# A two-layer graph network on one core: the running sums and the destination rows move from HBM into SBUF

## The reference

```python
# layer 0: attention
xl = h @ Wl + bl;  xr = h @ Wr + br;  e = edge_weight1 @ We
logits = leaky_relu(xl[src] + xr[dst] + e, 0.2) @ att
ex = exp(logits - segment_max(logits, dst)[dst]);  den = segment_sum(ex, dst)
out = segment_sum(xl[src] * (ex / den[dst])[:, None], dst)
h0 = batchnorm(gelu(h + out + bias));  x = x + h0
# layer 1: messages
em = relu(layernorm(concat(h[src], h[dst]) @ msg_w + msg_b)) * edge_weight
messages = segment_sum(em, dst) / count
x = x + gate * relu(layernorm(concat(h, messages) @ upd_w)) + (1 - gate) * h
```

## Time and profile before

| | |
|---|---|
| median of 3 runs | 2326.95 us (2321.8 to 2328.92) |
| profiled execution, own time | 2325.57 us |
| its span, first to last instruction | 2323.7 us |
| PE busy | 1608.6 us, 69% |
| DVE busy | 1539.4 us, 66% |
| ACT busy | 1027.0 us, 44% |
| POOL busy | 1646.2 us, 71% |
| moved by DMA | 233.58 MB |

### The profile page before, as it was taken

The page is one execution under the profiler, slowest core; times in us unless marked ns, Lnnn a source line. Parts: engine busy times, 40 slices in busy tenths (PEclk is TensorE's granted clock), DMA queues, the critical chain, the costliest instruction groups (busy, mean ns, idle before and its releaser), DMA issues.

```text
span 2323.7 us, 45075 instructions
## 1 busy us (share of the span) xinstructions
PE 1608.6 (69%) x10064; PEld 1151.3 (50%) x10064; DVE 1539.4 (66%) x5042; ACT 1027.0 (44%) x3827; POOL 1646.2 (71%) x1729
## 2 busy tenths in 40 slices
PE   5588787777777777777676776656566656656564
PEld 4366454555545555555465554444444444445443
DVE  6667665656565555655568886776666667676757
ACT  4444443444444444434454554444444444444435
POOL 5677777777777777777037777777777777777753
PEclk9799999999999999999778898998989899898997
DMA  8633333333333333333652343333333333333324
GB/s 222 181 99 98 96 96 88 96 89 95 88 96 92 93 95 88 95 88 77 158 166 70 98 106 96 87 95 87 95 87 94 91 91 86 93 96 88 93 63 111
DMA packets 222657, 233.58 MB, mean 101 GB/s; under 512 B 116266, under 2 KB 166332, under 8 KB 222533
## 3 DMA queue, kind: packets, MB, share of 16 engines
q0 software_dynamic: 55168, 114.83, 20.1%
q1 hardware_dynamic: 165958, 117.37, 18.8%
q10 hardware_dynamic: 1472, 0.73, 0.2%
HBM read 196.29 MB, written 36.46 MB: 100 GB/s over the span
## 4 chain that ended last, share of the span: by engine, by line
POOL 53%; issue 20%; PE 11%; DVE 7%; DMA 6%; ACT 1%; POOLq 1%; SPq 1%; DVEq 0%; ACTq 0%
POOL room L697 53%; DMA room<-src_table,rec 3%; PE psum L951 2%; PE psum L878 2%; PE psum L956 1%; PE psum L969 1%; DMA dst_table<-rows 1%; PE psum L778 1%; PE psum L860 1%; PE psum L850 1%; PE psum L843 1%; DMA room<-state 1%; DVE stats L1352 1%; DVE rows L1364 0%; PE psum L868 0%
## 5 line engine op out<-in xcount | busy, mean ns | idle before, releaser
L697 POOL DMA_INDIRECT room<-src_table,rec x1638 | 1573.8, 961 | 523.8 <-issue 486.1
L951 PE MATMUL psum<-room,ident 128*128 128x384 f32 (+1 forms) x512 | 273.1, 619 | 370.5 <-DMA room<-src_table,rec 313.9
L1242 ACT ACTIVATE room<-psum 128x128 f32<-128x128 f32 x832 | 219.0, 274 | 541.4 <-DVE room L1778 538.8
L1592 DVE TENSOR_TENSOR room<-psum,room 128x384 f32<-128x384 f32 (+1 forms) x256 | 151.2, 591 | 386.9 <-ACT room L1174 216.3
L1174 ACT ACTIVATE room<-psum 128x384 f32<-128x384 f32 (+1 forms) x256 | 131.8, 515 | 523.2 <-PE psum L850 516.9
L1778 DVE TENSOR_TENSOR room<-psum,msg_g 128x384 f32<-128x384 f32 (+1 forms) x256 | 151.0, 590 | 275.9 <-PE psum L956 267.6
L951 PEld LDWEIGHTS psum<-room,ident 128*128 128x128 f32 x512 | 85.7, 210 | 404.0 <-issue 363.7
L969 PE MATMUL psum<-room 128*125 128x128 f32 x1664 | 264.4, 302 | 1.6 <-ACT room L1254 1.6
L878 PE MATMUL psum<-room 128*125 128x128 f32 x1664 | 254.0, 293 | 16.5 <-ACT room L1192 10.6
L956 PEld LDWEIGHTS psum<-room 125*128 125x128 bf16 x2496 | 185.9, 108 | 129.5 <-issue 107.5
L1792 DVE SCALAR_TENSOR_TENSOR room<-room,rstd_e,msg_beta 128x128 f32<-128x128 f32 x832 | 242.5, 349 | 10.2
(11 more groups left out here) (224 smaller groups left out, 2228.6 us busy)
## 6 DMA issues: line engine op xcount, KB each, us to landing
room<-dst_perm SPq DMA_DIRECT2D x128, 416.0 KB
room<-src_table,rec POOLq DMA_INDIRECT x1638
room<-dst_table SPq DMA_DIRECT2D x128, 64.0 KB
src_table<-rows SPq DMA_DIRECT2D x24, 224.0 KB
dst_table<-rows SPq DMA_DIRECT2D x24, 224.0 KB
st_in<-state SPq DMA_DIRECT2D x64, 65.5 KB
st_in<-state SPq DMA_DIRECT2D x64, 64.0 KB
state<-st_out SPq DMA_DIRECT2D x64, 64.0 KB
```

What stands on the lines that cost most here:

```text
L697: pool.indirect_dma_start(out=xg[:, u, t * P:(t + 1) * P], out_offset=None, in_=table[:, :], in_offset=bass.IndirectOffsetOnAxis(ap=rec[:, ...
L951: nc.tensor.matmul(msg_bank[b][:, cols], ident[:, :], xg[:, u, t0 * P:t1 * P], start=True, stop=False, skip_group_check=True)
L1242: i = nc.scalar.activation(sq[:, j * P:(j + 1) * P], msg_bank[b][:, j * P:(j + 1) * P], ACT.Square, accum_out=var_e[:, c, j:j + 1])
```

## The change

- Nodes are laid out so that node n lies in partition n mod 125, column n / 125 (`(t p)` in place of `(p t)`). A window that begins at any node is then two neighbouring columns, split at a partition: the partitions from `left` on lie in the first column, those below it in the second.
- Destination rows stay in SBUF (`dst_rows`), and `dst_table` is gone. DVE picks the window out of the two columns (`nodes_of`, `pick_rows`), with a start column that it reads into a register.
- The states stay in SBUF (`held`, `held_den`, `held_max`, `cnt`), and `state0`, `state1`, `factor_rows`, their zeroing, their loads and stores and the reading back are gone. DVE merges into both columns (`gat_merge`, `gat_add`, `msg_add`). `held` shares its room with `feat_h`, so it is set to zero on POOL before loop 1 and on DVE before loop 2.
- `split_low` comes in block 2, not 3; the masks are written as bf16; the node's own part enters by transposes of `node_h`.
- At the end TensorE puts the own part into banks (`own_in_bank`) in another order around the wait for the last state: groups 2 and 3 into banks that the loop leaves free, 0 and 1 once DVE and ACT are through with theirs, 4 and 5 behind the first transposes of the sums.
- The chunk list has nine more small steps a block; x, x1, the source table and the output move in pieces of 512 bytes.

```diff
             def store_rows(n, g):
                     sp.dma_start(node_cols(src_table[n], p0, p1, t0, t1),
-                                 rows[p0:p1, g % 3, 0, 0:t1 - t0, :]).then_inc(s_src_out[g % 3], 16)
-                for p0, p1 in NODE_ROWS:
-                    sp.dma_start(node_cols(dst_table[n], p0, p1, t0, t1),
-                                 rows[p0:p1, g % 3, 1, 0:t1 - t0, :]).then_inc(s_dst_out[g % 3], 16)
+                                 rows[p0:p1, g % 3, 0:t1 - t0, :]).then_inc(s_src_out[g % 3], 16)
...
-            return table[0:N, :].rearrange("(p t) f -> p t f", t=NT)[p0:p1, t0:t1, :]
+            return table[0:N, :].rearrange("(t p) f -> p t f", p=PP)[p0:p1, t0:t1, :]
...
+            done = 10 * GT * PP
+            pool.wait_ge(s_proj, 10)
+            pool.memset(feat_room[:, 0:done], 0.0).then_inc(s_zero, 1)
+            pool.wait_ge(s_proj, NG)
+            pool.memset(feat_room[:, done:NC * D], 0.0).then_inc(s_zero, 1)
...
+            def start_of(u):
+                return starts_of(pair_info[0:1, u, 1:2])[0]
+            def nodes_of(s, k, u):
+                v = u % 2
+                base, left = (pair_info[:, u, i:i + 1].bitcast(F32) for i in (2, 3))
+                dve.wait_ge(s.dst[v], turns(s, k, v, 2, 32, last))
+                dve.tensor_scalar(side[:, u, 0:1], iota_p[:, :], left, None, ALU.is_ge)
+                dve.tensor_scalar(side[:, u, 1:2], iota_p[:, :], left, None, ALU.is_lt).then_inc(s.side, 1)
+                dve.wait_ge(s.side, k + 1)
+                dve.tensor_scalar(turned[:, :], side[:, u, 1:2], float(W), base, ALU.mult, ALU.add).then_inc(s.turned, 1)
...
+                dve.tensor_tensor(node_id[:, v:v + 1], turned[:, :], iota_p[:, :], ALU.add).then_inc(s.id, 1)
+            def pick_rows(s, k, u, start):
...
+                dve.tensor_scalar(dfar[0:W, :], rows_of[1], side[0:W, u, 1:2], None, ALU.mult).then_inc(s.far, 1)
+                dve.wait_ge(s.far, k + 1)
+                dve.scalar_tensor_tensor(out=dwin[0:W, v, :], in0=rows_of[0], scalar=side[0:W, u, 0:1], in1=dfar[0:W, :],
+                                         op0=ALU.mult, op1=ALU.add).then_inc(s.win, 1)
...
-            def msg_add(k, u):
+            def msg_add(k, u, start):
-                dve.wait_ge(s.st[v], turns(s, k, v, 2, 16, last))
+                dve.tensor_tensor(fac2[0:W, :], factor[:, bass.ds(start, 2)], side[0:W, u, :], ALU.mult).then_inc(s.fac, 1)
                 dve.wait_ge(s.sum, nth(k, NB))
-                dve.wait_ge(s_fac[v], (k - v) * 8 + 16)
-                dve.scalar_tensor_tensor(out=st_out[0:W, v, 0:D], in0=sum_bank[v][0:W, 0:D], scalar=fac_in[0:W, v:v + 1],
-                                         in1=st_in[0:W, v, 0:D], op0=ALU.mult, op1=ALU.add).then_inc(s.state, 1)
...
+                for j in range(2):
+                    rows_j = held[:, bass.ds(start + j, 1), :].rearrange("p a f -> p (a f)")
+                    i = dve.scalar_tensor_tensor(out=rows_j, in0=sum_bank[v][0:W, 0:D], scalar=fac2[0:W, j:j + 1],
+                                                 in1=rows_j, op0=ALU.mult, op1=ALU.add)
+                i.then_inc(s.state, 1)
...
-            for u in range(2):
-                sp.wait_ge(gat.kept[u], (last + U) * 8)
-                settle(sp)
-            for q, (t0, t1) in enumerate(PIECES):
-                for p0, p1 in NODE_ROWS:
-                    sp.dma_start(st_all[p0:p1, t0:t1, :], node_cols(state0, p0, p1, t0, t1)).then_inc(s_x[q], 16)
...
-            for g in range(NZ):
+            for g in (2, 3):
                 own_in_bank(g)
+            pe.wait_ge(msg.hg, nth(last + U, 0))
+            pe.wait_ge(msg.sq, nth(last + U, 0))
+            for g in (0, 1):
+                own_in_bank(g)
+            pe.wait_ge(msg.state, last + U)
             turn_msg(0)
+            turn_msg(1)
+            for g in (4, 5):
+                own_in_bank(g)
...
+            dve.wait_ge(s_u, NG)
+            dve.memset(feat_room[:, :], 0.0).then_inc(s_zero, 1)
```

More of the change, by code:

```diff
@@ L535, in slot @@
+                    two, three = two_chunks(k + 2)
                     if there(k, -3, end):
@@ L1260, in msg_slot @@
                     lagged(msg_relu, k, u, b, 1, end)
-                    if b == 0 and there(k, -1, end):
+                    if b == 1 and there(k, -1, end):
                         split_high(msg, k + 1, (u + 1) % U)
@@ L1503, in list_block, with step @@
-                dve.wait_ge(s_blk2, kb + 1)
+                steps = [0]
+                def step(i):
+                    steps[0] += 1
+                    i.then_inc(s_blk1, 1)
+                    dve.wait_ge(s_blk1, kb * LIST_STEPS + steps[0])
+                ge(dve, s_blk, kb * 2)
+                step(dve.tensor_scalar(hit, ends, k_col[:, :], None, ALU.is_le, ALU.add, accum_out=lcol[:, 0:1]))
+                step(dve.scalar_tensor_tensor(out=hit2, in0=iota_c[:, :], scalar=lcol[:, 0:1], in1=first, op0=ALU.is_equal,
+                                              op1=ALU.mult, accum_out=lcol[:, 1:2]))
@@ new lines, in list_block @@
+                step(dve.scalar_tensor_tensor(out=lcol[:, 2:3], in0=k_col[:, :], scalar=float(W), in1=lcol[:, 1:2],
+                                              op0=ALU.mult, op1=ALU.add))
+                dve.tensor_scalar(k_col[:, :], k_col[:, :], float(P), None, ALU.add).then_inc(s_blk, 1)
+                start, turn, left, off = (lcol[:, i:i + 1] for i in range(3, 7))
+                step(dve.tensor_scalar(start, lcol[:, 2:3], float(N), None, ALU.min))
+                step(dve.tensor_scalar(turn, start, 1.0 / W, None, ALU.mult))
@@ L1634, in gat_add @@
+                for j in range(2):
+                    rows_j = held[:, bass.ds(start + j, 1), :].rearrange("p a f -> p (a f)")
+                    dve.scalar_tensor_tensor(out=rows_j, in0=rows_j, scalar=eshift[0:W, j:j + 1], in1=part[0:W, j, :],
+                                             op0=ALU.mult, op1=ALU.add)
                 dve.drain().then_inc(s.state, 1)
             def gat_slot(k, u, end):
+                now = (u - 2) % U
                 for b in range(NB):
@@ L1640, in gat_slot @@
                     lagged(gat_max, k, u, b, 1, end)
+                    if b == 0 and there(k, -1, end):
+                        nodes_of(gat, k + 1, (u + 1) % U)
+                        pick_rows(gat, k + 1, (u + 1) % U, start_of((u + 1) % U))
                     if b == 1 and there(k, 2, end):
-                        gat_merge(k - 2, (u - 2) % U)
+                        start = start_of(now)
+                        gat_merge(k - 2, now, start)
                     if there(k, -1, end):
@@ L1680, in batch_stats @@
                 i.then_inc(s_bnst, 1)
-            done = 0
-            for q in range(NQ):
-                attention(q)
-                while done < NG and t_end(done) <= PIECES[q][0]:
-                    batch_stats(done)
-                    done += 1
-            for g in range(done, NG):
-                batch_stats(g)
+            dve.wait_ge(gat.state, last + U)
+            settle(dve)
+            link(dve.tensor_scalar(factor[:, :], held_den[:, :], 1e-16, None, ALU.add))
+            link(dve.reciprocal(factor[:, :], factor[:, :]))
+            link(dve.scalar_tensor_tensor(out=factor[:, :], in0=held_max[:, :], scalar=BIG / 10, in1=factor[:, :], op0=ALU.is_lt,
+                                          op1=ALU.mult))
+            for g in range(NG + 2):
+                if g < NG:
+                    attention(g)
+                if g >= 2:
+                    batch_stats(g - 2)
             dve.wait_ge(s_bnst, NG)
```

409 lines of the change are left out of this document (190 added, 219 removed).

## The result

The changed kernel takes 2299.59 us (median of 4 runs, 2296.81 to 2302.73), the kernel before 2327.39 (2321.8 to 2328.92): a ratio of 0.9878, 95% interval 0.9864 to 0.9891. Its profiled execution took 2299.76 us, with a span of 2297.9. The gathers first: page, part 5, and the timeline of POOL (start, length, what, wait) at the edges of the loops, as the earlier trace rows.

The account below looks back on a forecast made before the run. POOL's gathers were taken to bound both loops. Opening -4, loops 0 and 0, middle -18 and end -6 sum to -28 against 2325.57, so 2297.6; with the median 1.4 above, 2299 us, range 2286 to 2320.

Parts of the forecast that it names:

- So both loops run at POOL's pace: Both loops: a gather every 1.25 and 1.262 us sets the time; other engines' work stays hidden under some 16.4 us a pair.
- Opening, forecast -4: Before the first bulk gather: dropped `dst_table` stores end a 5.62 us wait, memsets add 5.7; -4 us, ends +1 and -6.
- Loop 1, forecast 0: Layer 0's gathers: DVE gains 4.2 us a pair, 13.8 of 16.3 busy, hidden behind POOL; 0 us.
- loop 2, 0: Layer 1's gathers: DVE's added work fits into its 4.2 us a pair of waiting for TensorE; 0 us.
- The step priced at +3.4 us a pair in loop 2, with 0.8 left: DVE in loop 2: new steps and two register reads add net 3.4 us a pair to 11.35 busy; the tightest place.
- Middle, forecast -18: Between the loops' gathers: no state read back from HBM, fewer stores; -18 us, ends -12 and -22.
- the way of the state: Middle: with the state kept in SBUF, `BATCH_NORM_AGGREGATE` comes at 1134.3 where it stood at 1149.62; -15 us.
- the projections: Middle: projections lose waits for `dst_table`, one of 5.84 us, but TensorE then sets the pace; -3 us.
- End, forecast -6: After loop 2: four own parts go ahead of the last state and TensorE no longer idles; -6 us, ends -3 and -9.
- The rival of DVE as the bound: Loop 2: DVE's added cost passes 4.2 us a pair, each us over costing 63; 2356 us, chance 0.1.
- Gathers beside DVE: Rival: DVE's new two-input SBUF steps stretch one gather a pair by 0.15 us, costing 19; 2318 us, chance 0.12.

Follow-up runs that it names:

- condition A: The first measurement: kernel before 2327.39 us, changed kernel 2299.59 us, ratio 0.9878.
- memset experiment: Changed kernel with POOL's 5000-column memset moved ahead of its wait for the list of destinations: 3146.8 us, ratio 1.0261 to the kernel before.
- the second store: Changed kernel without middle and low destination-row parts, plus another store of each group of rows to an unread table: 2984.2 us, ratio 0.9662.
- condition B: State of all twelve experiments, seen on three chips: kernel before 3063 to 3080 us, changed kernel 3164.6 us against 3072.1, ratio 1.0296.
- The light pair: Kernel before and changed kernel, both without the middle and low parts of the destination rows in TensorE's sums: 3029.5 us and 2968.4 us.
- the eight steps: Eight unneeded 128-column DVE steps added to each pair of loop 2: in the kernel before 3098.0 us, in the changed kernel 3177.2 us.

## Why the forecast held, point by point

- **The bound.** "So both loops run at POOL's pace" held in condition A: gathers 1.250 and 1.266 us apart, none that waits for `psum` longer than the usual 0.3 us between two gathers, mean 960 ns where it was 961.
- **Opening, forecast -4, measured -2.3.** A size was off. The list of destinations was issued at 58.70, 2.8 us sooner than 61.52, and not by the 5.62 of the one wait that the step counted; the memsets cost 5.7 as forecast. The memset experiment shows that they stand in the way, by 2.8 us; the second store, that the stores were worth about 4 us, give or take the scatter.
- **Loop 1, forecast 0, measured -1.8, and loop 2, 0 and +2.2.** The mean hides two things that nearly cancel: the usual distance of two gathers is 1.252 us in this profile and 1.249 in that of before (+2.4 us a loop), and fewer of loop 1's gathers are drawn out (6 over 1.05 us, where there were 34). The first is no effect of the change: the changed kernel in condition B has 1.249 again.
- **DVE.** The step priced at +3.4 us a pair in loop 2, with 0.8 left. DVE's busy time grew 2.1 and its idleness in the new steps by 1.0, 3.1 in all; the first read left DVE idle for 0.43 and the second not at all, where 0.75 each was taken. It waits 1.4 us a pair for TensorE, not 0.8. The room was mis-sized as well: the 4.2 us that DVE waits for TensorE are not all room, for a slot that nothing holds took 13.1 us, so there were 3.2. The slot grew by 2.2 and 1.0 is left. The room left came out near the 0.8 forecast because both terms were too large by about 1 us; that is luck. Had the slot grown by the 3.4 of the price, POOL would not have hidden it all.
- **Middle, forecast -18, measured -18.6.** The term has two parts: -15 for the way of the state, -3 for the projections. From the last gather to `BATCH_NORM_AGGREGATE` it went from 48.6 to 32.0, so -16.6; from there to x1's first gather nothing changed (25.5 and 25.6); then 36.0 became 33.8, -2.1. The light pair in condition B repeats the first part: from the last gather to x1's first 95.8 and 78.5. No run keeps the state in HBM with the rest of the change beside it, so that the 16.6 are the state's way is read from the waits that are gone, not from a run of its own; the stores' part was run, and gave about 2.
- **End, forecast -6, measured -5.3.** The last sum now comes 8.8 us after the last gather and not 7.6, a price of the fuller DVE that the step had not; the stretch behind it lost 6.4. The four own parts took 4.76 us, 1.2 each, near the slow pace of before, the last two 0.94 each. The step gave the gain to the order and the clock together; the runs give 1.7 us to the order, and only since the read of the state is gone. Of the 6.4, 4.4 are idleness of TensorE that is gone (it was busy for 10.1 of 14.5 us, now for all 8.0) and 2.0 are busy time, which the granted clock goes with (0.76 before, 0.87 now).
- **The rival of DVE as the bound** did not come true in condition A, by 1.0 us a pair. In condition B the kernel did end on the slower side, in loop 2, but the rival's mechanism is not shown: the eight steps make a slot in straight code 1.6 us longer (16.7 for 15.1), which by the rival's 63 pairs is 100 us, and they cost 13 to 22. What costs there is the change's work on DVE and TensorE's lateness together, since the loss is gone when TensorE has a third less, and halves when TensorE is let go a block sooner. Why added work can cost little is seen in part: it falls into DVE's waits for the late signals, which shrink (531.3 to 405.0 us, 391.6 to 119.8). Why TensorE is late stays open. Its pauses come at about the same place of a pair (at matmuls 46 to 52 in 56 pairs of the changed kernel, 34 to 48 in 56 of the kernel before with the eight steps), and not in the straight code behind the loop.
- **Gathers beside DVE.** The 128-column steps with two SBUF inputs drew no gather out enough to show in the mean. The wide ones of `own_part` still do: 1.22 and 1.23 us, here at the start of loop 2 in condition A.

```profile
1190.88 0.94 POOL L636 DMA_INDIRECT room<-src_table,rec  x1 [0.31 <-issue]
1192.13 1.22 POOL L636 DMA_INDIRECT room<-src_table,rec  x1 [0.30 <-issue]
1193.66 1.23 POOL L636 DMA_INDIRECT room<-src_table,rec  x1 [0.30 <-issue]
```

The Trainium skill ("SBUF — State Buffer", section Who interferes with whom) says that a DVE instruction with two SBUF inputs contends with a GpSimd instruction that reads SBUF. The wide steps have two such inputs, and the trace agrees in these rows; for the short ones the unchanged mean shows no price.

## What to carry to other kernels

Cut the span where the bounding engine starts and stops, and price a change in each piece by what ends last there: all five pieces came out within 2.2 us. An order of work that hides behind a wait is worth nothing until the wait ahead of it is gone, so test such edits in pairs. And say how much room is left in every loop that a change leans on: here 3.2 us of room became 1.0, which was free in one condition, while in another, where TensorE was late for a reason that no trace names, the same kernel lost 3%. Read that room from slots that nothing holds, not from one engine's waiting time, which was 4.2.

## What had not been expected of the hardware

The same two programs took 2327 and 2300 us in one condition, 3072 and 3165 in another, which three chips showed. In the slower one an instruction of POOL takes no longer (a gather 0.94 us, a memset 4.28), but TensorE stands up to 2.7 us between two matmuls, and its semaphores rise up to some 10 us behind the recorded ends of its matmuls, several at once; POOL's waits of 2.1 to 2.6 us in loop 1 and DVE's of some 6 in loop 2 end with them. TensorE's granted clock over the changed kernel was 0.76, not 0.89. A register read from SBUF held DVE for 0.43 us at one place of a pair and for nothing at the other.
